# Key projection ahead of half the values, later query sets between the first attention steps, and two DMA queues for the key writes: an attention and MoE-LoRA block on one core

## What is computed

```python
x = x + layernorm(attn(layernorm(x), wq, wk, wv, wo))     # no affine parameters
x = x + layernorm(ffn(layernorm(x), W_base, b_base, W_gate, A, B))

def attn(x):
    q = rope((x @ wq).reshape(4, 256, 32, 16))            # 32 query heads of 16
    k = rope((x @ wk).reshape(4, 256, 8, 16))             # 8 key and value heads, each for 4 query heads
    v = (x @ wv).reshape(4, 256, 8, 16)
    scores = q k^T / 4, causal mask, softmax in fp32
    return (softmax(scores) @ v) @ wo

def ffn(x):                                                # 8 experts of rank 16, the top two
    route_w = top-2 softmax gate of x @ W_gate^T, normalised
    return x @ W_base^T + b_base + sum_e route_w[e] * (x @ A[e]^T) @ B[e]^T
```

## Time and profile before

| | us |
|---|---|
| median of 3 runs (lowest, highest) | 241.3 (240.67, 242.18) |
| the profiled execution's own time | 241.24 |
| its span | 239.5 |
| busy: TensorE, VectorE, ScalarE, GpSimd | 201.5, 163.1, 135.8, 121.8 |

### The profile page before, as it was taken

The page is one execution under the profiler, slowest core; times in us unless marked ns, Lnnn a source line. Parts: engine busy times, 40 slices in busy tenths (PEclk is TensorE's granted clock), DMA queues, the critical chain, the costliest instruction groups (busy, mean ns, idle before and its releaser), DMA issues.

```text
span 239.5 us, 3788 instructions
## 1 busy us (share of the span) xinstructions
PE 201.5 (84%) x1292; PEld 123.5 (52%) x1304; DVE 163.1 (68%) x342; ACT 135.8 (57%) x238; POOL 121.8 (51%) x109
## 2 busy tenths in 40 slices
PE   0499999997787879999999969898879989998760
PEld 0494843444354544544444514144769868896640
DVE  1773525867878767668687621276898898888874
ACT  2231441242114697879667694872378387768781
POOL 8200232553339496979854756793666252423042
PEclk9999999999999999999999999999999999999995
DMA  5998046988897509673873233032241001110113
GB/s 171 355 371 310 0 155 194 219 273 283 166 240 261 98 1 299 137 167 54 162 115 74 43 59 86 12 90 49 61 91 36 3 0 44 44 48 0 45 44 131
DMA packets 34066, 29.88 MB, mean 125 GB/s; under 512 B 3968, under 2 KB 29568, under 8 KB 34048
## 3 DMA queue, kind: packets, MB, share of 16 engines
q1 hardware_dynamic: 33536, 29.52, 46.6%
q10 hardware_dynamic: 512, 0.13, 0.3%
HBM read 17.19 MB, written 10.09 MB: 114 GB/s over the span
## 4 chain that ended last, share of the span: by engine, by line
PE 38%; DVE 19%; ACT 17%; issue 7%; DMA 7%; SPq 5%; POOL 4%; ACTq 2%; POOLq 0%; DVEq 0%
PE ps L1110 6%; PE ps L1095 5%; ACT L559 5%; DVE stats L760 4%; PE ps L1069 4%; PE ps L1010 4%; ACT region_a L701 4%; PE ps L1000 3%; PE ps L1158 3%; DVE nmax L937 3%; PE ps L986 3%; DMA region_b<-q_scr 3%; PE ps L1133 2%; SPq L334 2%; DMA x_sb<-x 2%
## 5 line engine op out<-in xcount | busy, mean ns | idle before, releaser
L937 DVE TENSOR_REDUCE nmax<-ps 128x4 f32<-128x1024 f32 x32 | 39.2, 1224 | 14.1 <-PE ps L1069 13.9
L512 POOL TENSOR_SCALAR_AFFINE_SELECT region_a<-region_a 128x1024 f32<-128x1024 f32 x32 | 35.3, 1108 | 19.0 <-ACT region_a L701 18.7
L701 ACT ACTIVATE region_a<-ps 128x1024 f32<-128x1024 f32 x32 | 32.8, 1024 | 0.9 <-PE ps L1095 0.8
L1095 PE MATMUL ps<-region_b,kst 98*128 98x512 bf16 x96 | 27.5, 381 | 3.4 <-ACT region_a L701 2.0
L1000 PE MATMUL ps<-region_a,region_c 128*128 128x512 f32 x64 | 29.0, 598 | 0.0
L934 DVE TENSOR_REDUCE nmax<-ps 128x4 f32<-128x512 f32 x32 | 21.9, 683 | 6.8 <-PE ps L1053 6.4
L1110 PE MATMUL ps<-region_a,v_aug 128*32 128x512 f32 x192 | 25.3, 603 | 0.6 <-POOL region_a L512 0.6
L698 ACT ACTIVATE region_a<-ps 128x512 f32<-128x512 f32 x32 | 19.2, 600 | 8.6 <-PE ps L1095 8.2
L565 ACT ACTIVATE std<-mv,eps_sb 128x1 f32<-128x1 f32 x32 | 9.3, 293 | 23.5 <-DVE mv L761 23.3
L559 ACT ACT_TABLE_LOAD x17 | 21.8, 1283 | 1.1 <-PEq L1254 0.8
L440 POOL TENSOR_TENSOR region_a<-region_a 128x512 f32<-128x512 f32 x4 | 6.5, 1629 | 29.3 <-DVE region_a L808 29.3
(11 more groups left out here) (102 smaller groups left out, 426.0 us busy)
## 6 DMA issues: line engine op xcount, KB each, us to landing
region_b<-q_scr SPq DMA_DIRECT2D x8, 768.0 KB, 6.3
q_scr<-region_c SPq DMA_DIRECT2D x8, 384.0 KB, 3.5
x_sb<-x SPq DMA_DIRECT2D x8, 256.0 KB, 6.0
q_scr<-region_c SPq DMA_DIRECT2D x8, 256.0 KB, 3.4
attn_t<-o_sb SPq DMA_DIRECT2D x32, 64.0 KB, 2.3
rden_bc<-r_scr SPq DMA_DIRECT2D x8, 256.0 KB, 3.5
out<-region_b SPq DMA_DIRECT2D x8, 256.0 KB, 2.0
kst<-k_scr SPq DMA_DIRECT2D x8, 192.0 KB, 4.2
```

Of the source, the lines that this page charges most:

```text
L512: pool.affine_select(out=blocks, in_=blocks, compare_op=ALU.is_ge, fill=0.0, base=0, pattern=[[0, 2], [0, REP], [1, P]], channel_multiplie ...
L701: nc.scalar.activation(probs[:, u % PRING, 1:3, :], ps[:, 4:6, :], ACT.Exp, scale=float(HEAD_DIM) ** -0.5).then_inc(exp_done, 1)
L937: nc.vector.tensor_reduce(nmax[:, gi % 2, 1, heads], ps[:, 1:3, :].rearrange("p a (r k) -> p r a k", r=REP), AX.XY, ALU.max, negate=True). ...
L1095: last = nc.tensor.matmul(ps[:, 3 + j, :], kst[0:TROWS, slot, k, kt * P:(kt + 1) * P], qst[0:TROWS, slot, k * REP:(k + 1) * REP, qt * P:(q ...
```

## The change

- SP issues tiles 0 and 1 first, then the identity, tile 2, wv, tile 3 and the rest as before.
- VectorE normalises tile 0 right behind its own statistics; tile 1 follows the statistics of tile 2, as before.
- TensorE's order behind set 0: turn tiles 4 to 7, keys, values of tiles 4 to 7, set 2, the first 4 matmuls of set 3 (`FIRST_3`). The other 4 of set 3 and all 8 of set 4 are in steps 0 to 6 of the loop (`FILL`), 2, 2, 1, 1, 2, 2, 2 of them. Sets 2 and 3 change their banks.
- `rope(3, 0..2)` is at loop steps 2, 3, 4 on VectorE, behind the step's reductions.
- The writes of the keys' second half go to ScalarE's DMA queue, behind `copy_v(1)`, which is now behind the splits of sets 0 and 1. SP keeps the six of the first half.
- SP loads group 2's queries behind those of group 1.
- Set 4 is copied out at step 7 in place of 5, its additions are at step 8 on GpSimd behind the split of the maxima (`sum_late`), its splits at 11 and 13, its write at 15; group 5's loads are at step 16 in place of 15.

```diff
@@ -59,7 +59,7 @@
 MAX_STEP = {4 * gi + MAX_LAG - (gi == GROUPS - 1): gi for gi in range(GROUPS)}
-LOADS = {7: 4, 15: 5, 18: 6, 22: 7}
+LOADS = {7: 4, 16: 5, 18: 6, 22: 7}
 VECTOR_OUT = 5
@@ -68,10 +68,11 @@
 EARLY_OUT = {UNITS + 2: 0, UNITS + ST_LAG - 1: 1}
-ROPE_3 = {0: 1, 1: 2}
-MATMULS_4 = (1, 1, 1, 1, 1)
-ROTATE_4, SPLIT_HIGH_4, SPLIT_MIDDLE_4, WRITE_4 = 5, 10, 12, 14
+ROPE_3 = {2: 0, 3: 1, 4: 2}
+FIRST_3 = 4
+FILL = {0: (3, 4, 2), 1: (3, 6, 2), 2: (4, 0, 1), 3: (4, 1, 1), 4: (4, 2, 2), 5: (4, 4, 2), 6: (4, 6, 2)}
+ROTATE_4, SPLIT_HIGH_4, SPLIT_MIDDLE_4, WRITE_4 = 7, 11, 13, 15
 SPLIT_WEIGHTS = {15 + j: j for j in range(8)}
 CAT = DIM + EXPERTS * RANK + EXPERTS
@@ -259,7 +260,7 @@
         SETS = [(0, 0), "K", (0, 1), (1, 0), (1, 1)]
-        SET_BANKS = [(2, 3), (4, 5), (6, 7), (2, 3), (4, 5)]
+        SET_BANKS = [(2, 3), (4, 5), (2, 3), (6, 7), (4, 5)]
         set_of = {s: i for i, s in enumerate(SETS)}
         WRITES_Q = WRITES_K = 16 * 2 * len(RUNS)
@@ -281,19 +282,37 @@
             copy(o_sb[:, gi % 2, :, qt * P:(qt + 1) * P], ps[:, 6 + qt, :].rearrange("p (r n) -> p r n", r=REP))\
                 .then_inc(o_ready[gi >= VECTOR_OUT], 1)
+        def write_k(engine, part, half):
+            i = set_of["K"]
+            first, count = RUNS[part]
+            dst = k_scr[half].rearrange("(s i f) h n -> i (f h) s n", s=TERMS, i=2)
+            for ri in range(2):
+                if part == 0:
+                    engine.wait_ge(part_h, 2 * i + 1 + ri)
+                elif part == 1:
+                    engine.wait_ge(part_m, 2 * i + 1 + ri)
+                else:
+                    engine.wait_ge(part_l[ri], i + 1)
+                rows = parts[half * 64:half * 64 + 64, i % 2, ri, part:part + 1, :]
+                engine.dma_start(dst[ri, :, first:first + count, :], rows.broadcast_to([64, count, HALF]))\
+                    .then_inc(k_written[half], 16)
         block = ctx.enter_context(nc.Block())
         @block.sync
         def _(sp):
             sp.dma_start(x_sb[:, 0, :], x[0:P, :]).then_inc(x_loaded[0], 16)
-            sp.dma_start(ident_sb[:, :], ident).then_inc(ident_loaded, 16)
-            sp.dma_start(wv_sb[:, :, :], wv.rearrange("(c p) n -> p c n", p=P)).then_inc(wv_loaded, 16)
             wq_v = wq.rearrange("(c p) n -> p c n", p=P)
             for t in range(1, TILES):
                 if t == 4:
                     sp.dma_start(wq_sb[:, :, 0:256], wq_v[:, :, 0:256]).then_inc(wq_loaded[0], 16)
                 sp.dma_start(x_sb[:, t, :], x[t * P:(t + 1) * P, :]).then_inc(x_loaded[t], 16)
+                if t == 1:
+                    sp.dma_start(ident_sb[:, :], ident).then_inc(ident_loaded, 16)
+                if t == 2:
+                    sp.dma_start(wv_sb[:, :, :], wv.rearrange("(c p) n -> p c n", p=P)).then_inc(wv_loaded, 16)
             sp.dma_start(tab_sb[:, :, :], tables).then_inc(tab_loaded, 16)
             sp.dma_start(wk_sb[:, :, :], wk.rearrange("(c p) n -> p c n", p=P)).then_inc(wk_loaded, 16)
             sp.dma_start(wq_sb[:, :, 256:512], wq_v[:, :, 256:512]).then_inc(wq_loaded[1], 16)
@@ -318,22 +337,6 @@
                         sp.dma_start(dst[ri, :, first:first + count, half * HALF:(half + 1) * HALF],
                                      parts[:, i % 2, ri, 0:count, :]).then_inc(scr_written[i], 16)
-            def write_k(part, half):
...
             def wait_ring(gi):
                 if gi >= RING:
@@ -387,14 +390,13 @@
             write_q(0)
             load_q(0)
-            load_q(2)
             for part in range(PARTS):
-                for half in range(2):
-                    write_k(part, half)
+                write_k(sp, part, 0)
             load_k(0)
             load_k(1)
             write_q(2)
             load_q(1)
+            load_q(2)
             load_k(2)
             load_k(3)
             load_q(3)
@@ -455,6 +457,8 @@
                 for j, (val, table) in enumerate(((re, cos), (im, sin), (re, sin), (im, cos))):
                     pool.tensor_tensor(late_mul[:, j, :].rearrange("p (b n) -> p b n", b=2), val, table, ALU.mult)\
                         .then_inc(late_multiplied, 1)
+            def sum_late():
                 for i, op in enumerate((ALU.subtract, ALU.add)):
                     pool.wait_ge(late_multiplied, 2 * i + 2)
                     pool.tensor_tensor(late_rot[:, i, :], late_mul[:, 2 * i, :], late_mul[:, 2 * i + 1, :], op)\
@@ -531,6 +535,8 @@
                     pool.tensor_copy(high, full).then_inc(nmax_high, 1)
                     pool.wait_ge(nmax_high, gi)
                     pool.tensor_tensor(low, full, high, ALU.subtract).then_inc(nmax_split, 1)
+                if n == ROTATE_4 + 1:
+                    sum_late()
                 if n in DIVIDE:
                     divide(DIVIDE[n])
                 if n in ATTN_LOW:
@@ -617,12 +623,14 @@
             copy_v(0)
             for t in range(4, TILES):
                 copy_xnt(t)
-            split_high(0)
-            split_middle(0)
-            copy_v(1)
-            for i in range(1, 4):
+            for i in range(4):
                 split_high(i)
                 split_middle(i)
+                if i == 1:
+                    copy_v(1)
+                    write_k(act, 0, 1)
+                    write_k(act, 1, 1)
+                    write_k(act, 2, 1)
             def normalise(k, t, dst, src, ready):
                 nc.scalar.activation(dst, src, ACT.Identity, scale=rstd[:, k, t:t + 1],
@@ -781,7 +789,9 @@
             for t in range(TILES):
                 dve.wait_ge(x_loaded[t], 16)
                 ln_stats(0, t, x_sb[:, t, :])
-                if t >= 1:
+                if t == 0:
+                    input_norm(0)
+                if t >= 2:
                     input_norm(t - 1)
             input_norm(TILES - 1)
@@ -828,7 +838,6 @@
             for i in range(3):
                 for step in range(3):
                     rope(i, step)
-            rope(3, 0)
             def invert(gi):
@@ -974,9 +983,9 @@
             def project(i, first=0, count=2 * KC):
-                if i >= 3:
-                    pe.wait_ge(rope_mul, i - 2)
+                if i in (2, 4):
+                    pe.wait_ge(rope_mul, i // 2)
                 if SETS[i] == "K":
                     pe.wait_ge(wk_loaded, 16)
                     pe.wait_ge(xnt_ready, TILES)
@@ -990,7 +999,7 @@
                 else:
                     half, g = SETS[i]
                     pe.wait_ge(wq_loaded[g], 16)
-                    if i == 2:
+                    if i == 3:
                         pe.wait_ge(v_ready, 2)
                     pe.wait_ge(xnt_ready, 4 * half + 4)
@@ -1022,11 +1031,13 @@
             turn_and_project_v(0)
             project(0)
-            turn_and_project_v(4)
-            for i in range(1, 4):
-                project(i)
-            project(4, 0, 2 * KC - sum(MATMULS_4))
+            for t in range(4, TILES):
+                turn_x(t)
+            project(1)
+            for t in range(4, TILES):
+                project_v(t)
+            project(2)
+            project(3, 0, FIRST_3)
             def scores(n):
@@ -1038,7 +1049,7 @@
                     pe.wait_ge(bf_const, 2)
                     pe.wait_ge(v_ready, 2)
-                    pe.wait_ge(rope_mul, 4)
+                    pe.wait_ge(rope_mul, 3)
                     pe.wait_ge(pool_const, 4)
                 else:
                     pe.wait_ge(s0_free, n)
@@ -1103,6 +1114,9 @@
                 b, g = divmod(gi, 2)
                 qt, kt = ((0, 0), (1, 0), (1, 1))[piece]
                 pe.wait_ge(probs_masked, 4 * gi + 4)
+                if gi == 0:
+                    pe.wait_ge(rope_mul, 4)
                 if gi >= 1 and kt == 0:
                     wait_o(pe, 2 * gi - 1 + qt)
                 for j in range(GROUP_KV):
@@ -1203,9 +1217,9 @@
                     scores_t(n - ST_LAG)
                 if n < UNITS:
                     scores_more(n)
-                if n < len(MATMULS_4):
-                    project(4, 2 * KC - sum(MATMULS_4[n:]), MATMULS_4[n])
+                if n in FILL:
+                    project(*FILL[n])
                 if n in MAX_STEP:
                     turn_max(MAX_STEP[n], n)
                 gi, r = divmod(n - PV_LAG, 4)
```

13 lines of the change are left out of this document (removed).

## The result

| | before | after |
|---|---|---|
| median of 4 runs (lowest, highest) | 241.13 (240.67, 242.18) | 247.03 (245.97, 248.35) |
| the profiled execution's own time, its span | 241.24, 239.5 | 248.10, 246.4 |
| busy: TensorE, VectorE, ScalarE, GpSimd | 201.5, 163.1, 135.8, 121.8 | 205.6, 165.3, 135.5, 121.3 |

What follows compares the result with a forecast made beforehand. The head was bound by TensorE's queue up to 54 us and set 2's chain up to 66.24, later steps by TensorE. 241.24 + 1.4 - 1.75 = 240.9 us, no difference to be told; range 237.2 to 243.6.

Steps and rivals of the forecast that it cites:

- D: Lead won in the input stage: TensorE's unbroken work begins 1.5 to 2.0 us earlier, taken as 1.75.
- Set 2, first write to load: SP's writes of set 2 up to issuing load_q(1): 6.0 us as for set 0, 7.3 as other end.
- Set 2, the load: load_q(1), awaited by step 4: lands 6.3 us after issue, at 64.6 - D; load_q(2) behind doesn't stretch it.
- Steps 4 to 7: Loop with filling of two at steps 4, 5, 6: a step costs 0.7 us more; turn_max at 73.45 - D.
- Rival (C): Input stage: D only 0.9, slow TensorE pace ends when it did or tile 2 lands no sooner; 241.7 us, chance 0.13.
- Steps 0 to 7: Loop walk: 1.7 + D won at step 4, less by 3.2 us at step 7; shift 1.55 - D.
- the load, even at 65.9, costs 0.4 at most: Step 4: scores(4) at 64.6, its reduction at 65.5, so a late query load costs at most 0.4 us.
- the order of the projections: Ahead of the loop: keys end 3.15 + D us earlier, set 2 only D - 0.6 earlier.
- GpSimd's late set: Steps 7 on: GpSimd's multiplications and maxima split end at 81.75, turn_max(1) wants them at 82.0 - D; cost 0 to 0.5 us.
- (D): ScalarE's six key writes take 1.37 us each, reductions start 1.9 later; decides from 1.05 an issue; 242.8 us, chance 0.16.
- (B): Filling of two in the loop steps costs nothing, shift 2.1 us less; 238.8 us, chance 0.26.
- The load for step 20: load_q(5) lands at 105.7 - D, scores(20) wants it at 107.0 - D: slack 1.3 us, no cost.

Runs made afterwards that it cites:

- a1: Changed kernel with GpSimd's memset of the key operand's last rows held until all tiles are normalised; 244.94 us, ratio 1.0179 to the kernel before.
- a2: Changed kernel plus 6 useless fp32 matmuls on TensorE at the end of step 3, in the gap; 243.09 us, ratio 1.0098 to the kernel before.
- a5: Changed kernel with all twelve key writes on SP's queue again; 246.73 us, ratio 1.0249 to the kernel before.
- d2: Changed kernel with all key writes on SP and the values of tiles 4 to 7 projected behind set 2; 242.40 us, ratio 1.0069.
- e1: Kernel before plus useless bf16 matmuls on TensorE in steps 5 to 13; 241.35 us, ratio 1.0053 to the kernel before.
- a3: Changed kernel with the last 7 matmuls of set 4 all at step 3, in the gap; 242.57 us, ratio 1.0083 to the kernel before.
- d1: d2 with the memset held, set 3 wholly ahead of the loop, set 4 two matmuls a step in steps 0 to 3, its old later timing; 244.48 us.
- d3: d1 plus useless bf16 matmuls on TensorE, three a step in steps 4 to 8, one in 9 to 13; 240.37 us, ratio 1.0014.
- a4: Changed kernel with group 2's query load put back directly behind group 0's; 248.33 us, ratio 1.0315 to the kernel before.

## Why the prediction was wrong, step by step

Counted at turn_max(0): forecast 73.45 - 1.75 = 71.7, measured 78.5. The misses add up to 6.65 of the 6.8 us between them:

| step of the prediction | forecast | measured | miss |
|---|---|---|---|
| Input stage, D | 1.75 | 0.25 | 1.5 |
| Set 2, first write to load | 6.0 | 7.8 | 1.8 |
| Set 2, the load | 6.3 | 6.65 | 0.35 |
| Steps 4 to 7, forecast at full clock | 8.85 (64.6 to 73.45) | 11.9 (66.63 to 78.52) | 3.0 |

**Input stage.** The bytes and the order in VectorE's queue were right (in a1 TensorE's unbroken work begins at 7.70, forecast 8.1 to 8.6). The step that failed was to price the first normalisation at the 0.55 of a row that stood after 8.1 us, and to move it to 4.9 without a look at what GpSimd does there. The row of the memset was in the trace of before, ending at 7.32. Rival (C) gave D as 0.9 for two other reasons, and neither made this miss: VectorE stood beside the memset. But what it says of the slow pace at the start is a real spread: in the six traces of the changed input stage with its memset (after, a2 to a5, d2) the second transposes start at 9.89 each time, and set 0 between 16.25 and 17.41. That is 1.2 us from how long the slow pace lasts, and 0.25 is the low end of it. The 1.75 was also counted against a trace in which the second tile's data came late (7.13, and 5.95 in e1): part of it was never the change's to win.

**Set 2 and step 4.** The step that failed is the write's term: 6.0 was set 0's and the 7.3 was named as the other end; the choice of the lower end was wrong, and even the upper one was short by 0.5. The 7.3 had been laid to the key loads beside it, but without them it is longer, 7.7 to 7.8 in six traces; the tail of the last write is unexplained.

**Steps 0 to 7.** The walk by steps was right as far as work and waits go: a2 shows its pace of 2.9 us. What failed is the sentence that "the load, even at 65.9, costs 0.4 at most". The forecast's own numbers had TensorE done with its filling at 61 and scores(4) at 64.6, all less D, so a gap of more than 3 us stood in them, where the kernel before had one of 1.32. Measured, it was 5.92. I priced the gap by its length alone and never asked what the clock does behind it. That is 3.2 us by the rows and 3.1 by a2 (8.75 in place of 11.89), the largest term of the miss; it was no rival, so the range could not hold it.

**Right:** the order of the projections to 0.3 us once D is set; the first reduction and the pace of steps 0 to 3; GpSimd's late set not binding at turn_max(1). Of the rivals, (D) is refuted by its price (0.76 us an issue, 1.05 needed), so the kernel is slower as (D) had it but not by its cause, and (B), filling for nothing, by a2's steps of 2.9 us and by a3, which has less filling and turn_max(0) 3.1 us sooner. The load for step 20 had 1.3 us of slack in the forecast and made TensorE wait for 0.53.

Why the change doesn't pay even without these: a3 has no long gap, and even its faster pair of runs (241.4 and 241.8, mean clock 0.992 and 0.988) is no better than the kernel before (241.06 on that chip). What follows on this is argued from the rows. In both kernels set 2 stands behind the keys and all the values, so their order among themselves hardly moves it, and the time that the keys gain is not wanted, since VectorE's queue holds set 2 ahead of the first reduction in any case. Putting set 2 ahead of half the values (d2) brings step 4 forward the most, to 61.85, with the changed input stage as it is; and there the filling (d2) or the thin steps behind it (d1) take the gain back, or the matmuls that hold the clock do (d3). How much of that remainder is due to which is not settled.

## What to carry to other kernels

When a plan leaves TensorE idle ahead of a wait, or leaves several steps thin, price also the work behind it at half clock, and read the granted clock by windows before any other explanation; useless work put into the gap (a2), with the steps behind it timed from their own start, shows within one run what the clock is worth. The record of the granted clock isn't all, though: it reads 1.00 from 10 to 15 us in the kernel before, where four transposes take 1.12 us that later take 0.60. When an instruction is moved, look at what the other engines do at its new place, VectorE and GpSimd above all. A lead at one end of the kernel is worth only what the next wait lets through, so follow one fixed event (here turn_max) through both traces. And a lead against one trace of the kernel before holds what chance gave or took in that trace: look at the same rows in a second trace of the same code.

## What the runs showed of the hardware

- A useless 5.3 us of matmuls made the kernel 3.9 us faster (a2; 3.1 of it between step 4 and turn_max(0)), and 20 short ones 4.1 us faster (d3 against d1); on a kernel whose clock is full they cost 0.5% [1.0012, 1.0094] (e1).
- The clock fell to 0.50 for 13 us with no TensorE wait over 1.74 us (d1).
- The slow pace of TensorE's first matmuls lasts differently from run to run: with the second transposes at 9.89 in six traces, set 0 started between 16.25 (a4) and 17.41 us (after). The granted clock reads 1.00 there.
- VectorE's normalisation of 128x512 took 2.70 us beside a GpSimd memset on only 2 partitions, and 0.55 without it; its statistics row of 0.69 (3.43 to 4.12), also beside the memset, was not longer.
- The last write of set 2 (128 KB) landed 4.84 us after its issue, and for about the last 2 us of it the DMA engines moved 25 GB/s at most, after 300 to 400. The whole chain of set 2's writes took 7.7 to 7.8 us in the six traces with no key loads just before it, and 6.4 to 7.3 in the eight with them.
